# Two-layer transformer kernel: layer-0 projection weights landed by a casting DMA, and the first exp of the layer-1 attention in two halves

## What is computed

```python
x = L0_attn_x
xn = _layernorm(x, axis=-1)
s = _L0_attn_ref(xn, Wq, bq, Wk, bk, Wv, bv, Wo, bo)   # rope, 16 heads, causal softmax
g = _silu(_L0_ffn_ref(xn, w_gate, w_up, w_down))       # int32 weights / 127, hidden 3072
x = x + s * g
xn = _layernorm(x, axis=-1)
s = _L1_attn_ref(xn, ...)                              # one head of width 1024
g = _silu(_L1_ffn_ref(xn, W, b, ids, weights))         # 8 adapters mixed by weights
x = x + s * g
```

## Time and profile before

| | us |
|---|---|
| the two runs shown | 3113.61 and 3247.44, median 3180.52 |
| the profiled execution, its own time | 3112.94 |
| its span (slowest core, 7) | 3111.4 |
| spans of its 8 cores | 3094.5 to 3111.4 |
| PE busy in the span | 2283.8 (73%) |
| DVE busy | 884.0 (28%) |
| ACT busy | 878.4 (28%) |
| POOL busy | 65.2 (2%) |

### The profile page before, as it was taken

The page is one execution under the profiler, slowest core; times in us unless marked ns, Lnnn a source line. Parts: engine busy times, 40 slices in busy tenths (PEclk is TensorE's granted clock), DMA queues, the critical chain, the costliest instruction groups (busy, mean ns, idle before and its releaser), DMA issues.

```text
span 3111.4 us, 40058 instructions; the slowest of 8 cores (3094.5 to 3111.4 us)
## 1 busy us (share of the span) xinstructions
PE 2283.8 (73%) x15302; PEld 1248.9 (40%) x15302; DVE 884.0 (28%) x1695; ACT 878.4 (28%) x1239; POOL 65.2 (2%) x124
## 2 busy tenths in 40 slices
PE   3799999974567545697777777609678877887877
PEld 1344444432233213364664666406357323333333
DVE  4444444431222254434223111250110002112122
ACT  4111111112221235464444444312110224222222
POOL 0011110000000000000000000000000000000000
PEclk8899999996787765656556555659889988887898
DMA  6122222102101010101000100162316012011010
GB/s 160 22 33 33 31 36 36 21 1 68 34 28 34 27 27 28 54 10 59 5 2 28 35 2 1 46 190 87 71 54 210 1 28 54 17 38 54 1 55 27
DMA packets 62013, 136.03 MB, mean 44 GB/s; under 512 B 8057, under 2 KB 16251, under 8 KB 59268
## 3 DMA queue, kind: packets, MB, share of 16 engines
q1 hardware_dynamic: 40964, 105.15, 10.5%
q0 software_dynamic: 20864, 28.32, 6.4%
HBM read 142.88 MB, written 18.88 MB: 52 GB/s over the span
## 4 chain that ended last, share of the span: by engine, by line
PE 57%; ACT 15%; DVE 13%; issue 7%; DMA 6%; DVEq 0%; SPq 0%; ACTq 0%; PEldq 0%; POOLq 0%
PE PS L924 8%; PE PS L758 7%; ACT EB L946 7%; PE PS L1234 5%; PE PS L619 5%; PE PS L628 5%; PE PS L1397 5%; PE PS L1466 4%; PE PS L662 4%; PE PS L1202 3%; DVE PS L929 2%; ACT PRJ L766 2%; PE PS L1323 2%; DVE ACC L673 2%; PE PS L990 1%
## 5 line engine op out<-in xcount | busy, mean ns | idle before, releaser
L924 PE MATMUL PS<-Q,K 64*128 64x128 bf16 x2176 | 274.1, 304 | 124.4 <-ACT EB L946 119.3
L946 ACT ACTIVATE EB<-PS,negBh 128x1152 bf16<-128x1152 f32 (+7 forms) x128 | 204.0, 1594 | 257.2 <-DVE PS L929 241.9
L924 PEld LDWEIGHTS PS<-Q,K 64*128 64x128 bf16 x2176 | 211.5, 135 | 153.9 <-issue 143.2
L1234 PE MATMUL PS<-XN,W1FULL 128*128 128x512 bf16 x768 | 179.6, 389 | 58.0 <-DVEq L95 18.2
L662 PE MATMUL PS<-HT,WDT 128*128 128x512 bf16 x768 | 194.4, 390 | 35.5 <-DVE HT L645 21.9
L758 PE MATMUL PS<-XN,WBLK 128*128 128x512 bf16 x768 | 210.8, 443 | 10.1 <-DVE Q L773 5.1
L929 DVE TENSOR_TENSOR PS<-PS,trinegT 128x128 f32<-128x128 f32 x256 | 76.6, 300 | 439.2 <-PE PS L924 434.3
L619 PE MATMUL PS<-XN,WGT 128*128 128x512 bf16 x768 | 172.1, 383 | 26.7 <-DVE XN L444 20.1
L1202 PE MATMUL PS<-identw,PLAND 128*128 128x128 f32 x1024 | 131.2, 292 | 81.6 <-DMA PLAND<-Wsel 71.5
L628 PE MATMUL PS<-XN,WUT 128*128 128x512 bf16 x768 | 169.7, 379 | 0.0
L1202 PEld LDWEIGHTS PS<-identw,PLAND 128*128 128x128 f32 x1024 | 128.5, 207 | 85.4 <-issue 84.4
(11 more groups left out here) (161 smaller groups left out, 2518.8 us busy)
## 6 DMA issues: line engine op xcount, KB each, us to landing
PLAND<-Wsel SPq DMA_DIRECT2D x64, 512.0 KB, 4.4
XF<-xT SPq DMA_DIRECT2D x8, 1024.0 KB, 12.7
XT<-xT SPq DMA_DIRECT2D x4, 2048.0 KB, 10.1
x1park<-XT SPq DMA_DIRECT2D x32, 256.0 KB
X1CH<-x1park SPq DMA_DIRECT2D x8, 1024.0 KB, 9.0
XT<-x1park SPq DMA_DIRECT2D x4, 2048.0 KB, 8.0
outT<-XT SPq DMA_DIRECT2D x32, 256.0 KB
LAND<-wu POOLq DMA_DIRECT2D x16, 256.0 KB, 3.7
```

The costliest lines, as they stand in the source:

```text
L924: tS = P.op("tensor", lambda t, h=h, gi=gi, tt=tt, off=off: t.matmul(PS[:, off + tt * 128:off + (tt + 1) * 128], head_k(h, ts(tt, 128)), h ...
L946: s.activation(EB2[:, slot, 0:klen], PS[:, 0:klen], AF.Exp, bias=negBh[:, h:h + 1]), inc=True)
L1234: tk = P.op("tensor", lambda t, fc=fc, j=j, n=n: t.matmul(BK(n), W1FULL[:, j, ts(fc, 128)], src_xn[:, j, ts(n, 512)], start=(j == 0), stop ...
```

## The change

Two edits that have nothing to do with each other.

In `stage_T`, the two half-piece DMAs on SP's queue and the two casts on ACT are replaced by one DMA of 128x1024 on POOL's queue that reads f32 and writes bf16 straight into the landing slot. It waits for the transposes that last read this slot (`land_guard[li]`). FLND and `cvt67` go. The transposes wait for the DMA's own semaphore.

In `l1_frontA`, the exp of 2048 columns becomes two of 1024, the first behind the last matmul of bank 1, the second behind that of bank 3.

```diff
-    FLND = ar.place("FLND", [128, 2, 512], F32, oW + (36 << 10))
...
-    cvt67 = {0: None, 1: None}
...
         def stage_T(fc):
             li = fc % 4
             sl = fc % 2
-            cvt = None
-            for h in range(2):
-                P.wait("sync", cvt67[h])
-                t_half = P.dma("sync", FLND[:, h, :],
-                               W_d[fc * 128:(fc + 1) * 128,
-                                   h * 512:(h + 1) * 512], sem=f"dp{h}")
-                P.wait("scalar", t_half)
-                P.wait("scalar", land_guard[li])
-                cvt = P.op("scalar", lambda s, li=li, h=h: s.copy(
-                    LANDY(li)[:, h * 512:(h + 1) * 512], FLND[:, h, :]),
-                    inc=True)
-                cvt67[h] = cvt
-            t_land = cvt
+            P.wait("gpsimd", land_guard[li])
+            t_land = P.dma("gpsimd", LANDY(li),
+                           W_d[fc * 128:(fc + 1) * 128, :], sem=f"dl{li}")
             P.wait("tensor", t_land)
...
             tQK = P.op("tensor", lambda t, gi=gi, n=n: t.matmul(
                 BK(n), NQSQ_ROW[0:1, ts(gi, 128)], onesrow[0:1, 0:512],
-                start=False, stop=True), inc=(n == 3))
+                start=False, stop=True), inc=(n == 1 or n == 3))
+            if n == 1:
+                tQK1 = tQK
+        P.wait("scalar", tQK1)
+        P.op("scalar", lambda s: s.activation(
+            SSB[:, 0:1024], PS[:, 0:1024], AF.Exp))
         P.wait("scalar", tQK)
         tSc = P.op("scalar", lambda s: s.activation(
-            SSB[:, :], PS[:, 0:2048], AF.Exp), inc=True)
+            SSB[:, 1024:2048], PS[:, 1024:2048], AF.Exp), inc=True)
```

## The result

The changed kernel takes 3080.63 us (median of 11 runs; before 3113.48, median of 10). The forecast was 3081.

A forecast was written before the change was run, and what follows sets the result against it. No single engine was taken as the bound: a chain of waits alternates through all engines. Terms 15.4 + 3.2 + 0.8 + 5.5 + 2 + 4.7 = 31.6 us off 3112.9 gave 3081 us, range 3062 to 3108.

The forecast's parts named there:

- Blocks of K and Q: Layer-0 projections: at 12 places PE's idleness falls from 6.34 to 5.06 us without the casts, 15.4 us gained.
- Clock: Matmuls of the K and Q blocks: less idleness shifts TensorE's granted clock, 2 us gained, bounds -8 to +10.
- Start of V: First V matmuls: both pieces already landed, so transposes run back to back, 3.2 us gained.
- Blocks of V: V projection blocks: casts were already hidden, taken as 0, at most 0.35 us gained per block.
- Start of Q: First Q transposes: second group no longer waits for ACT's cast, 0.8 us gained.
- Start of K: First K matmuls: two pieces land beside the tables on another queue, at 716; 5.5 us gained, range 1 to 9.
- Exp: First tile of the four layer-1 attention groups: first half runs under matmuls; 4.7 us including table load, bounds 0 to 5.5.
- Table load: Very first layer-1 attention tile: ACT's table load goes under the matmuls, 1.28 us within the 4.7; no drain seen.
- Rival A: POOL's weight transfers come late: 3142 us in full (chance 0.03), 3087 if only K's start is late (0.07).
- Rival B: K and Q blocks: TensorE keeps its upper clock through the shorter gap, 21 us more, 3062 us; chance 0.05.
- Rival C: Layer-0 attention's clock settles lower, 0.50 instead of 0.56, up to 74 us more, 3155 us; chance 0.04.
- Rival D: Only attention part and starts gain, ACT's casts having covered another wait in the blocks: 3099 us; chance 0.09.

The follow-up runs named there:

- the kernel that kept both: Kernel before, FLND, SP's DMAs and ACT's casts kept, loads and casts of piece fc+2 placed ahead of block fc's copies: ratio 0.9938, 3095.7 us.
- exp-only kernel: Kernel before with only the layer-1 attention exp split in halves, no casting DMA: ratio 0.9992 (0.9981 to 1.0002).
- DMA-only kernel: Kernel before with only the casting DMA, the exp left whole: ratio 0.9904, about 3084 us.
- the two that only enter later: Kernel before with three or six repeats of DVE's last small copy ahead of the layer-1 attention: 3116.56 and 3114.91 us, one execution each.

## Why the prediction was right, point by point

The time (3081; measured medians of 3080.6 and 3077.2, and 3079.0 in the profiled execution) and the sign are right, and the main mechanism is shown. The closeness of the number is luck. Of the 31.6 us forecast, the changed stages gave 26.7: the projections 19.8 instead of 26.9, the layer-1 attention 6.9 instead of 4.7. The other 8.4 us of the 35.0 between the two spans came from stages that the forecast put at nothing. All differences here are from the slowest core of each kernel; starts of matmuls are those of the chain.

- *Blocks of K and Q, 15.4 us.* Measured 7.6 (K, start of block 0 to start of block 7: 109.6 to 102.0) and 7.8 (Q: 109.8 to 102.0), together 15.4, but for this term and the clock term of 2 together. The hand-overs gave 13.9: each is 1.08 to 1.17 shorter, not 1.28, because PE's transposes start 5.17 to 5.26 us behind the block and not the 5.06 of the matmuls of block 7 that gave the price. The matmuls themselves gave the rest, 0.7 us in K and 0.8 in Q. That the order in ACT's list was the cost, and neither the casts nor SP's DMAs, is shown by the kernel that kept both.
- *Clock, 2 us.* Measured 1.5, in the same 15.4. The sign of error that the forecast had set, matmuls of a block outside 7.8 to 9.25 us, did come: four of the twelve took 9.32 to 9.42. The spread had been read from too few blocks; the kernel before already has one of 9.35.
- *Start of V, 3.2 us.* Measured 3.4. The pattern read from the Wo stage carried over to a hundredth; the sum had set the end of the transposes against a timeline row of the matmuls, which begins 0.2 us before that end.
- *Blocks of V, 0.* From block 0 to block 7 it is 114.9 before and 115.1 after.
- *Start of Q, 0.8 us gained.* Measured 0.8 lost: the staging gained 0.6, but the last block of V before it met the lower clock level for longer and took 9.32 us instead of 7.87.
- *Start of K, 5.5 us.* The term that was mis-sized: 1.5, close to the bound of 1 that was given. The step that failed is "I take landing at 716, between the ends": the first piece landed at 719.5, 12.2 us after its issue, close to the 12.5 that the forecast's own upper bound gave for 3 MB. Four pieces and two tables were in flight together. Taking the tables away makes it 5.9 us, which shows the contention; the value between the ends had no row to stand on.
- *Exp, 4.7 us.* The idleness at the four first tiles fell by 2.13 + 3 x 0.86 = 4.7 us, as forecast. The stage fell by 6.9 on the slowest core and by 9.9 in the mean; in the exp-only kernel the time fell by only 2.5 and the mean over cores by 2.6, and the changed kernel's mean is 5.0 below the DMA-only one's. What goes beyond the 4.7 is the clock at the start of the groups, as the DMA-only kernel and the two that only enter later show. That it adds to this change rather than takes away is nothing that the forecast knew.
- *Table load.* It went under the matmuls. The exp follows it by 0.01 us; the page of the Trainium skill (ScalarE: Activation LUTs, What ACT_TABLE_LOAD costs) gives 1283 ns for the load, which the row has, and a drain of 1380 ns, which no row here has.
- *What was not forecast.* 6.8 us came from the layer-1 projections on the slowest core, 2.9 in the mean. The three large weight loads landed 1.5 to 3.3 us sooner each than on core 7 before (23.6, 15.6 and 13.8 us against 26.2, 18.9 and 15.3). But core 5 of that same execution before had 22.5, 15.5 and 13.7, so this is a difference between cores of one execution and no effect of the change that these runs show.

Rival A (late transfers) fell: within the blocks PE waited for a DMA on none of the eight cores. Its mild form, only the start of K late, is what happened at the start of K. The Trainium skill's rule (SBUF — State Buffer, the "DVE blocks DMA" trap) may hold, but three blocks of lead hid whatever it did, and no run here shows it. Rival B (the clock stays up) fell at 5.26 us of idleness, and also at 2.88 with transposes ahead of the matmuls. Rival C: the layer-0 attention stayed at 837 us, at a granted clock of 0.56. But its idea, that a stage's clock depends on how it is entered, fits the layer-1 attention, whose mean with unchanged code lay between 505.1 and 511.5 us. Rival D fell.

## What to carry to other kernels

A cheap instruction that stands in a strict list behind a wait costs its time wherever another engine waits for it. Look first for another place in the list; here that gave two thirds of the gain with no other edit. Ask of each wait which buffer it protects: PE waited for a multiply when it needed only the copies before it, and that one line was worth more than the whole change. And the length of a stage whose engine keeps falling idle can move by about one per cent with its entry time alone, so an edit worth less than that is judged by the wait it removes, or by the mean over cores and many executions, and not by one profile of the stage.

## What the runs showed of the hardware that was not expected

- The length of the layer-1 attention, with the same instructions, was 497.1 to 518.1 us over the cores of five kernels (before, DMA only, casts early, both late entries), and 523.2 on one core whose last group ran at a granted clock of 0.75; the other query groups took from 119.4 to 136.2. Delaying its entry by some 2 and 4 us went with a mean of 507.7 and 505.1 instead of 510.4, in one execution each.
- After the same 2.86 us of idleness TensorE kept 2.4 GHz through four banks of scores in one kernel (9.5 us) and fell to 1.2 GHz for two of them in another (14.4 us).
- TensorE can run the first instructions after 2.88 us of idleness at 2.4 GHz (eight transposes in 0.61 us) and fall to 1.2 GHz within the work that follows; such blocks took about 8.76 us, longer than those that began low (7.7 to 8.1).
- The first of four casting DMAs of 512 KB issued together landed in 5.9 us; with 2 MB of plain DMA from another queue beside them in 12.2 us.
